# Up weights split early, first query products ahead of the rope keys, keys summed on POOL, latents turned in halves

## The reference, cut to what matters

```python
q_c = _rms_norm(x @ wq_down.T, q_norm_w)                 # 384 channels
q_nope = (q_c @ wq_up.T).reshape(bs, seq_len, NH, D_NOPE)
q_pe = (q_c @ wq_rope.T).reshape(bs, seq_len, NH, D_ROPE)
kv_c = _rms_norm(x @ wkv_down.T, kv_norm_w)              # 128 channels
kv_up = (kv_c @ wkv_up.T).reshape(bs, seq_len, NH, D_NOPE + D_V)
k_rope_shared = (x @ wk_rope.T).reshape(bs, seq_len, 1, D_ROPE)
q_pe = _apply_rope(q_pe, cos, sin)
k_rope_shared = _apply_rope(k_rope_shared, cos, sin)
```

## Time and profile before

| | |
|---|---|
| runs shown, median | 925.0 us of 3 (923.31 to 925.41) |
| profiled execution, its time and its span | 922.51 us, 920.4 us |
| TensorE busy in the span | 844.5 us, 92% |
| VectorE, ScalarE, POOL busy | 567.2, 501.8, 218.7 us |
| mean granted TensorE clock | 0.969 |
| TensorE busy from 30.27 us to the first S step at 83.08 us | 43.7 of 52.8 us |
| `stage` from the first weights' issue (9.1 us) to landing | 9.7 us |
| `acc` from its issue (9.6 us) to landing | 13.5 us |

### The profile page before, as it was taken

How to read it: one execution, slowest core, us unless ns; L and a number is a source line. 1 busy time by engine, 2 the same in 40 slices (tenths; PEclk the granted TensorE clock), 3 DMA queues, 4 the chain that set the end, 5 groups by cost and what they waited for, 6 DMA issues and landing times.

```text
span 920.4 us, 13297 instructions
## 1 busy us (share of the span) xinstructions
PE 844.5 (92%) x4302; PEld 718.5 (78%) x4302; DVE 567.2 (62%) x1098; ACT 501.8 (55%) x1329; POOL 218.7 (24%) x231
## 2 busy tenths in 40 slices
PE   7978999999999986788887699999999999999997
PEld 5767888888788775577766487888888988889896
DVE  4654653753753668587987965635566665666467
ACT  5415744753753752688787552416374664837250
POOL 0212230230131134133232100160223222321330
PEclk9979999999999997999999799999999999999999
DMA  8022211311221001040330221173465464654432
GB/s 317 8 81 62 109 46 36 120 40 40 79 81 40 30 20 38 1 144 3 139 125 0 70 69 46 53 250 99 149 197 173 163 233 139 207 172 138 126 103 80
DMA packets 33678, 92.66 MB, mean 101 GB/s; under 512 B 6736, under 2 KB 12656, under 8 KB 32480
## 3 DMA queue, kind: packets, MB, share of 16 engines
q1 hardware_dynamic: 22352, 53.81, 18.2%
q0 software_dynamic: 11280, 38.25, 12.8%
HBM read 63.73 MB, written 20.97 MB: 92 GB/s over the span
## 4 chain that ended last, share of the span: by engine, by line
PE 64%; DVE 12%; issue 12%; ACT 8%; POOL 2%; SPq 1%; DMA 1%; ACTq 0%; POOLq 0%; DVEq 0%
PE ps L1309 51%; ACT Pt L675 3%; PE ps L1324 3%; PE ps L1641 2%; DVE kb_lo L865 2%; PE ps L1369 2%; ACT kb_hi L612 2%; PE ps L1631 1%; PE ps L1453 1%; DVE zx_lo L865 1%; DVE negmax L936 1%; SPq L435 1%; DVE acc L952 1%; POOL Pt L489 1%; ACT zx_hi L612 1%
## 5 line engine op out<-in xcount | busy, mean ns | idle before, releaser
L489 POOL TENSOR_TENSOR Pt<-Pt,rowinv 112x448 f32<-112x448 f32 x64 | 59.9, 935 | 271.1 <-DVE rowinv L943 270.7
L675 ACT ACTIVATE Pt<-ps,negmax 112x112 f32<-112x112 f32 x256 | 87.2, 357 | 21.6 <-DVE negmax L936 21.4
L1309 PE MATMUL ps<-x2T_hi,ws_hi 128*128 128x448 f32 x256 | 95.6, 373 | 0.6 <-DVE x2T_lo L865 0.6
L1309 PE MATMUL ps<-x2T_lo,ws_hi 128*128 128x448 f32 x256 | 94.2, 368 | 0.0
L1309 PE MATMUL ps<-x2T_hi,ws_lo 128*128 128x448 f32 x256 | 94.0, 367 | 0.0
L800 ACT ACTIVATE hf<-ps,b 128x448 f32<-128x448 f32 x64 | 40.6, 635 | 93.0 <-PE ps L1309 92.4
L1309 PE MATMUL ps<-w_hi,h_hi 128*128 128x512 f32 x224 | 89.0, 397 | 0.0
L1309 PE MATMUL ps<-w_hi,h_lo 128*128 128x512 f32 x224 | 87.9, 392 | 0.0
L1309 PE MATMUL ps<-w_lo,h_hi 128*128 128x512 f32 x224 | 87.6, 391 | 0.0
L865 DVE TENSOR_TENSOR h_lo<-hf,h_hi 128x448 fp32r<-128x448 f32 x64 | 39.9, 624 | 48.8 <-ACT h_hi L801 48.6
L1201 DVE TENSOR_TENSOR acc<-ps,acc 128x512 f32<-128x512 f32 x56 | 38.6, 690 | 42.6 <-PE ps L1309 41.8
(11 more groups left out here) (283 smaller groups left out, 2333.8 us busy)
## 6 DMA issues: line engine op xcount, KB each, us to landing
stage<-in_wf SPq DMA_DIRECT2D x32, 513.0 KB, 3.9
rows_in<-zero SPq DMA_DIRECT2D x30, 256.0 KB, 3.2
xs<-rows_in POOLq DMA_DIRECT2D x29, 256.0 KB, 4.3
rows_out<-yb POOLq DMA_DIRECT2D x29, 256.0 KB, 2.7
stage<-in_wa SPq DMA_DIRECT2D x4, 1408.0 KB, 6.1
stage<-in_wb SPq DMA_DIRECT2D x4, 1280.0 KB, 5.5
qr<-ro_hi SPq DMA_DIRECT2D x64, 56.0 KB, 1.9
qr<-ro_lo SPq DMA_DIRECT2D x64, 56.0 KB, 1.9
```

The costliest lines, as they stand in the source:

```text
L489: nc.gpsimd.tensor_tensor(p, p, rowinv[0:S, b % 2, :].unsqueeze(2).broadcast_to([S, GH, S]), ALU.mult).then_inc(norm_done, 1)
L675: last = nc.scalar.activation(Pt[0:S, b % 2, h * S:(h + 1) * S], ps[0:S, b % 2, h * S:(h + 1) * S], ACT.Exp, bias=negmax[0:S, b % 2, h:h + 1],
L1309: ins = mm(dst, w, x, start=start and i == 0, stop=stop and i == len(ops) - 1, skip_group_check=not (start and stop))
```

## The change

TensorE's, ScalarE's and VectorE's lists for group 0 are now three different ones and take in what stood ahead of them. The turns of the latents are items LAT, four batches each; the key products are items KR, one per half, and come behind A 0, A 1, E 0 and O 0. Those four items take banks 0 to 3, free after the turns of the first half. The split of `wa` comes right behind the first round of squares, its low part on VectorE. The rotated keys are added, copied to high (a product with a column of ones) and subtracted to low on POOL, with one buffer for each half. SP's first pack waits for all key products. The second half of the latents is normalised behind A 0 to O 0. VectorE's wait for `acc` moves to where it is read.

```diff
-ATT_PRE = [("E", 0), ("O", 0), ("A", 0), ("R", 0), ("E", 1), ("A", 1), ("A", 2), ("O", 1), ("Q", 0, 0),
-           ("R", 1), ("Q", 1, 0), ("Q", 2, 0), ("Q", 3, 0), ("Q", 0, 1), ("G", 0), ("SB", 0), ("Q", 1, 1)]
+_lat0, _lat1 = [("LAT", b) for b in range(HB)], [("LAT", b) for b in range(HB, B)]
+_kvn = [("VAL", b) for b in range(HB, B)]
+_q = [("Q", 1, 0), ("Q", 2, 0), ("Q", 3, 0), ("Q", 0, 1), ("G", 0), ("SB", 0), ("Q", 1, 1)]
+ATT_PRE = _lat0 + [("A", 0), ("A", 1), ("E", 0), ("O", 0), ("KR", 0)] + _lat1 + [
+    ("KR", 1), ("A", 2), ("E", 1), ("O", 1), ("Q", 0, 0)] + _q
+ATT_PRE_ACT = _lat0 + [("RMS", 1), ("A", 0), ("A", 1)] + _kvn + [("R", 0)] + _lat1 + [
+    ("A", 2), ("Q", 0, 0), ("R", 1)] + _q
+ATT_PRE_DVE = _lat0 + [("RMS", 1), ("A", 0), ("A", 1), ("E", 0), ("O", 0), ("NAT", 1), ("KR", 0)] + _lat1 + [
+    ("KR", 1)] + _kvn + [("A", 2), ("E", 1), ("O", 1), ("Q", 0, 0)] + _q
+PRE_BANK = {("A", 0): 0, ("A", 1): 1, ("E", 0): 2, ("O", 0): 3}
...
-ATT_POOL_PRE = [("O", 0), ("R", 0), ("O", 1), ("R", 1)]
+ATT_POOL_PRE = [("O", 0), ("R", 0), ("KR", 0), ("KR", 1), ("O", 1), ("R", 1)]
...
         n = places.index(item)
-        if n >= 2:
+        if places is self.pre and item in PRE_BANK:
+            return Place(PRE_BANK[item] - 6, number + n, None, None)
+        if n >= 2 and places[n - 2] not in PRE_BANK:
...
+        one = sb("one", [P, 1])
...
+        rope_keys = (krt, sT)
...
             load_b(0)
+            sp.wait_ge(kr_done, 4)
             pack(0, 0)
...
-            for i, (lo, hi) in enumerate(A_PIECES):
-                pool.wait_ge(a_hi, i + 1)
-                nc.gpsimd.tensor_tensor(wa_lo[:, lo:hi], stage[:, lo:hi], f32(wa_hi[:, lo:hi]),
-                                        ALU.subtract).then_inc(a_lo, 1)
-
+            nc.gpsimd.memset(one[:, :], 1.0).then_inc(one_set, 1)
+            pool.wait_ge(one_set, 1)
...
+                elif kind == "KR":
+                    cols = slice(j * HALF, (j + 1) * HALF)
+                    rot = rope_keys[j]
+                    pool.wait_ge(kr_mul, j + 1)
+                    nc.gpsimd.tensor_tensor(rot[:, 0, :], rot[:, 0, :], rot[:, 1, :], ALU.add).then_inc(kr_rot, 1)
+                    pool.wait_ge(kr_rot, j + 1)
+                    nc.gpsimd.tensor_tensor(kr_hi[:, cols], rot[:, 0, :], one[:, :].broadcast_to([P, HALF]),
+                                            ALU.mult).then_inc(krh, 1)
+                    pool.wait_ge(krh, j + 1)
+                    nc.gpsimd.tensor_tensor(kr_lo[:, cols], rot[:, 0, :], f32(kr_hi[:, cols]), ALU.subtract)\
+                      .then_inc(krl, 1)
...
+            squares(0)
+            act.wait_ge(in_lo, 2 * KD + 2)
+            act.wait_ge(st_ld, 16)
+            for lo, hi in A_PIECES:
+                copy(wa_hi[:, lo:hi], stage[:, lo:hi]).then_inc(a_hi, 1)
+            for b in range(HB):
+                values(b)
...
+            rms(0)
+            latents(0)
+            for i, (lo, hi) in enumerate(A_PIECES):
+                dve.wait_ge(a_hi, i + 1)
+                low(wa_lo[:, lo:hi], stage[:, lo:hi], wa_hi[:, lo:hi]).then_inc(a_lo, 1)
+            for b in range(HB):
+                values(b)
...
-            dve.wait_ge(acc_ld, 16)
...
             def add_output(at, t, free):
                 dve.wait_ge(job_done, at.number + 1)
+                dve.wait_ge(acc_ld, 16)
...
+                elif kind == "KR":
+                    for s in range(2):
+                        dve.wait_ge(kr_done, 2 * j + s + 1)
+                        ins = nc.vector.tensor_tensor(batches(rope_keys[j][:, s, :]),
+                                                      batches(ps[:, 2 * j + s, 0:HALF]), table(2 + s), ALU.mult)
+                    ins.then_inc(kr_mul, 1)
...
+            def rope_key(half):
+                pe.wait_ge(in_lo, 2 * KD + 2)
                 for s in range(2):
                     bank = 2 * half + s
-
-                    pe.wait_ge(tr_lo, bank + 1)
+                    item = ("A", s) if half == 0 else ("EO"[s], 0)
+                    pe.wait_ge(a_free[item[0]], AJ.count(item, 0))
...
+                if isinstance(g, int) and g == 0:
+                    pe.wait_ge(tr_lo, HB if item in PRE_BANK else B)
```

More of the change, by code:

```diff
@@ L269, in build @@
         wd = sb("wd", [P, KD, 768], at=first)
+        junk = sb("junk", [P, B, D], BF16, at=first)
+        sb("over_ro", [P, 9216 - 8704], at=first)
         xT_hi, xT_lo = pair("xT", [P, KD, T], first)
@@ L628, in _, with squares @@
             copy(maskb[0:S, :], maskf[0:S, :]).then_inc(const_done, 1)
-            for r in range(2):
+            def squares(r):
                 for b in range(HB * r, HB * r + HB):
@@ L640, in _, with values @@
                                      ss_eps[0:S, HB * r:HB * r + HB, :], ACT.Sqrt).then_inc(root_done, 1)
[L641 to L655, removed]
+            def values(b):
+                act.wait_ge(nat_done, b + 1)
+                copy(kvN_hi[0:S, b, :], nat[0:S, b % 4, QR:QR + LAT]).then_inc(kvn_hi, 1)
+            squares(0)
[5 more added lines that the diff above has]
+                values(b)
             def layernorm_root(i, r):
@@ L696, in att_step @@
                     ins.then_inc(a_job_hi[kind], 1)
+                elif kind == "LAT":
+                    act.wait_ge(tr_done, j + 1)
+                    copy(qkT_hi[:, :, j * S:(j + 1) * S],
+                         ps[:, j, 0:4 * S].rearrange("p (c s) -> p c s", c=4)).then_inc(tr_hi, 1)
+                elif kind == "RMS":
+                    squares(j)
+                elif kind == "VAL":
+                    values(j)
                 elif kind == "G":
@@ L882, in _, with rms @@
             dve.wait_ge(c_ld, 64)
-            for r in range(2):
+            def rms(r):
                 rows = slice(HB * r, HB * r + HB)
@@ L900, in _, with values @@
                     ins.then_inc(nat_done, 1)
[L901 to L908, removed]
+            def values(b):
+                dve.wait_ge(kvn_hi, b + 1)
+                low(kvN_lo[0:S, b, :], nat[0:S, b % 4, QR:QR + LAT], kvN_hi[0:S, b, :]).then_inc(kvn_lo, 1)
+            rms(0)
[5 more added lines that the diff above has]
+                values(b)
             def table(i):
@@ L1011, in att_step @@
                     ins.then_inc(a_free[kind], 1)
+                elif kind == "LAT":
+                    dve.wait_ge(tr_hi, j + 1)
+                    cols = slice(j * S, (j + 1) * S)
+                    low(qkT_lo[:, :, cols], ps[:, j, 0:4 * S].rearrange("p (c s) -> p c s", c=4),
+                        qkT_hi[:, :, cols]).then_inc(tr_lo, 1)
+                elif kind == "RMS":
+                    rms(j)
+                elif kind == "NAT":
+                    latents(j)
+                elif kind == "VAL":
+                    values(j)
+                elif kind == "KR":
[4 more added lines that the diff above has]
+                    ins.then_inc(kr_mul, 1)
                 elif kind == "SA":
@@ L1349, in _ @@
                         .then_inc(kr_done, 1)
-                if half == 0:
-                    for b in range(HB, B):
-                        turn_latents(b)
-            pe.wait_ge(tr_lo, B)
             def heads(ap):
@@ L1406, in att_step @@
                     bank = ps[:, 6 + at.bank, :]
+                if kind == "LAT":
+                    turn_latents(j)
+                    return
+                if kind == "KR":
+                    rope_key(j)
+                    return
+                if isinstance(g, int) and g == 0:
+                    pe.wait_ge(tr_lo, HB if item in PRE_BANK else B)
                 if kind in "EO":
```

11 lines of the change are left out of this document (4 added, 7 removed).

## The result

The changed kernel takes 916.6 us (median of 12 runs, 911.39 to 921.14), the kernel before 922.57 us (12 runs, 921.12 to 925.54). The ratio is 0.9924 with a 95% interval of 0.9900 to 0.9949: 7.0 us faster by the ratio, 6.0 by the medians. The forecast was 3.6 us faster. Of the 4.8 us between 921.4 and 916.6, 2.4 are the base: the three runs shown had a median of 925.0, twelve have 922.57. The other 2.4 are gain.

The account below looks back on a forecast made before the run. The start was taken as bound by the pack transfers' fixed 13.7 us chain to Q (3,0), TensorE behind it. 8.1 - 3.0 - 1.5 = 3.6 us gain: 922.5 to 918.9, or 921.4 against the 925.0 median; range 917.0 to 923.7.

Parts of the forecast that it names:

- the base: Starting time: the profiled execution's 922.5 us, 2.5 under the 925.0 median of runs shown; forecast 918.9, or 921.4 against that median.
- The path: From SP's first pack issue: 11.6 us to ScalarE's R 1, 13.7 to TensorE's Q (3,0), whatever any engine's speed.
- Full clock, 8.1 us: SP's first pack issues at 52.2 instead of 60.33 us, behind both keys' products: 8.1 us gained at full clock.
- The clock, 3.0 and 1.5 us: Half clock on TensorE after idles before A 0 and before Q (3,0), losing 3.0 and 1.5 us; chance 0.44.
- The bound of 4.5 for a long first fall: Upper bound of the loss to half clock after the idle before A 0: half as long again as 3.0 us.
- The case for one fall only: Rival: only one of TensorE's two idles before S 0 brings half clock; gain 5.1 or 6.6 us, chance 0.34.
- Part 1: Up weights' copies in ScalarE's early idleness, low parts on VectorE in about 4.0 us plus value splits: cost nothing.
- Part 4: Keys' sum, copy and split on POOL, 3.5 us a half, under 13 us of cover before G 0: nothing.
- Part 5: VectorE's four value splits beside POOL's KR 1: 0.8 to 3.5 us, O 1 up to 1.9 late, absorbed before Q (3,0).
- The sum itself: Whole-kernel gain: 8.1 - 3.0 - 1.5 = 3.6 us, with nothing changed behind Q (3,0).
- a rival, at 1 us either way: Both falls long, gain 0.6 us, 924.4; later clock dips fall differently, 1 us either way; chance 0.10.
- The slower rival: Clock low over A, E, O and both KR, past 18 us: packs start later, 4.5 us slower, 929.5; chance 0.06.

Follow-up runs that it names:

- keys first: Changed kernel with both key products moved ahead of A 0, A 1 and A 2: 909.57 us, ratio 0.9863 to the kernel before.
- ninth execution: Ninth profile of the unaltered changed kernel, with no half clock between 30 and 84 us: 913.88 us.
- first execution: First profile of the unaltered changed kernel, with one 6.8 us stretch of half clock from 34 us: 916.62 us.
- first of before: First profile of the kernel before, nothing changed, with half clock from 55 us (3.4) and 62 us (6.8): 922.51 us.
- second execution: Second profile of the kernel before, nothing changed, with half clock from 56 and 63 us (3.4 each): 923.36 us.
- third execution of before: Third profile of the kernel before, nothing changed, with half clock from 40, 53.5 and 74 us (3.4 each): 925.74 us.
- the one with the packs shared: Changed kernel with eight of the 16 transfers of pack (0,0) issued by ScalarE beside SP's eight: 913.38 us, ratio 0.9897.

## Why the prediction was right or wrong

**The path.** Right. The first pack comes at kr_done 4, and from the first pack it is 11.6 us to R 1 and 13.7 to Q (3,0), 13.67 to 13.69 in all three executions of before and all nine of the changed kernel, at every clock. It is no constant of the chip: in keys first, with SP alone too, it was 14.7. Issuing the transfers on two queues shortened it to 11.6 us. Between executions without half clock this is worth 2.0 us from the turn to S 0 (71.81 - 29.53 = 42.28 against 44.28), and 2.5 to 3.2 us in the timed runs; that shows the cause.

**Full clock, 8.1 us.** Right, small by 0.4. The ninth execution has 44.28 us from the turn to S 0 against 52.81: 8.5 us. For this stretch the forecast without falls was 44.7.

**The clock, 3.0 and 1.5 us.** Right for the usual execution: six of nine have both falls and 48.7 to 49.0 us from the turn to S 0, where the forecast was 49.2 (83.08 - 3.6 - 30.27). The first execution, with one fall only, is not the usual one. The single prices are right too: the first execution lost 3.1 us against the ninth, and Q (3,0) to S 0 takes 10.5 to 10.6 us with a second fall and 9.0 to 9.1 without. The bound of 4.5 for a long first fall was also met (50.48 less the second fall's 1.6 is 4.6 over 44.28). The case for one fall only leaned on a first idle "no longer than 1.70", where the prediction's own working had 1.8; it was 1.73, and eight of nine executions fell behind it. Why a fall comes in one execution and not in the next no row here shows. The Trainium skill, "TensorE: Matmul & The Clock Gate", section "The HAM clock gate", says that the monitor's counting runs free of the kernel's start, so that the same kernel changes clock at different points from run to run. The nine profiles are in line with that; none of them tests it.

**Part 1.** Right: VectorE's pieces took 3.2 us, 0.8 under the upper row, and were hidden.

**Part 4.** Right: with the keys back on VectorE and ScalarE the ratio was 0.9919 against 0.9924.

**Part 5.** Right in kind: four splits took 2.60 us, between the bounds of 0.8 and 3.5, and delayed O 1 by 0.64 us, which the idle before Q (3,0) absorbed. The Trainium skill's rule of an exclusive lock between POOL's reads and VectorE's two SBUF inputs ("SBUF — State Buffer", "Who interferes with whom") is borne out by 2.60 beside POOL and 0.89 without it. Its upper bound of three whole POOL instructions was not reached: the first split began at 55.40, 0.16 us ahead of POOL, and the last was through at 58.00, as POOL's third instruction (57.92) began.

**What failed.** Two steps: the base, and what lies behind S 0.
- "It lies 2.5 under the median of the runs shown, 925.0; against that median the forecast is 921.4." The three runs lay high; twelve give 922.57, beside which the profiled execution was an ordinary one. Put on that base, the forecast would have read 919.0 and its range 914.6 to 921.3, with 916.6 inside. This is half of the miss.
- The sum itself, 3.6 us for 6.0. Up to S 0 it holds: from the turn to S 0 the six usual executions take 3.9 to 4.1 us less than the first of before. What it had wrong lies behind S 0, which it put at nothing: "so time won before the first S step (83.08 us) should arrive at the end nearly whole", with the later dips of the clock only in a rival, at 1 us either way. From S 0 to the end of the span the nine profiles of the changed kernel take 835.6 to 839.1 us, mean 837.1, the three of before 837.3 to 839.6, mean 838.3. These 1.2 us go with the clock: the stretches of half clock behind S 0 add up to 37.5 to 53.1 us in the nine, mean 44.0, and to 46.0 to 52.9 in the three, mean 49.9, and within the nine the execution with 53.1 takes 3.1 us longer than the one with 37.5. Whether the change has a part in there being less of it stays open; three profiles of before are few. The last 0.8 us is not located: the six usual executions have a median time of 917.45, the twelve timed runs 916.6.

The term for the clock was that of one execution with both falls, and a median over executions also holds those with fewer. With seven of nine profiles showing both, this moves the median little. Three of the twelve timed runs lie at 911.4 to 911.9, 5 us under the bulk, which is what two falls cost (3.1 + 1.6). The ninth profile, without a fall, is also the shortest of the nine, at 913.88; that the three runs were such executions is argued, not shown. For single executions the lead does arrive within the scatter behind S 0: the ninth is 8.5 us ahead from the turn to S 0 and 8.6 at the end against the first profile of before.

**The slower rival** found nothing for it: the longest stretch of half clock was 10.2 us, not 18. And one thing I had not seen in the rows of before: its own two falls cost it nothing at S 0, for they lie ahead of Q (3,0), which waits for the packs. In all three executions the first pack comes 30.0 to 30.1 us behind the turn, whatever the clock does. In its second execution the second fall was half as long, TensorE reached Q (3,0) earlier and stood idle 1.80 us there instead of 0.33, for the same packs. So I was right to compare chains and not to credit the change with falls undone; but this had to be argued and was not.

## What to carry to other kernels

Find the chain with a fixed length (here 16 transfer issues and a landing, 13.7 us), ask what starts it, and move ahead of its start only what it needs; the order with both key products ahead of the A products gained about twice what the change did over the kernel before (13 us by the medians, where the change gained 6). Put a forecast on a base of many runs, or state it as a difference. Where an idle of TensorE may bring half clock, weigh all outcomes, and allow for the stages behind the change: their clock moved the time by up to 3 us here. An edit that closes such an idle can be worth more than the idle: 1.5 us of idle gave 3.0 to 4.4.

## What the hardware showed that I had not expected

- The stretches of half clock in the table are 3.4, 6.8 or 10.2 us long and nothing between, and an idle of 1.73 us was followed by one in eight of the nine profiles of the changed kernel, but not in the ninth and not in the one with the packs shared.
- Long products right behind the idle did not prevent the fall (one execution, 3.4 us).
- A fall needs no long idle: in the third execution of before the clock fell at 40 us among the late turns, with no idle over 0.56 us since the first turn at 29.72.
- POOL's copy as a product with a column of ones took 0.93 us for 128x448 with VectorE quiet, against 1.15 for two full operands.
- ScalarE issued eight transfers in 5.3 us beside SP's eight in 5.0: the two queues hardly held each other up.
